# The feed-forward half of a cross-attention block as one program instead of four, with shared buffers and split DMA queues

## The chip, the cores and the metric

The kernel runs on one core of one Trainium2 chip. Its time is the device time of one execution in microseconds (us). Three runs of the kernel before gave 2516.38, 2515.7 and 2514.28 us, a median of 2515.7 us.

## What is computed

`x` is 8192 rows (4 x 2048) of 512 numbers. The first half of the reference is a layer norm and a cross-attention in which each row looks at four rows of a table; the change does not touch it. The second half is a quantised feed-forward network on the normalised rows:

```
x = act_qdq(x)                                   # 16-bit integers times one scale for the whole tensor
up = act_qdq(x @ lpbq_dequant(w_up).T)           # 512 -> 1536
gate = act_qdq(x @ lpbq_dequant(w_gate).T)       # 512 -> 1536
sig = fixed_qdq_u16(jax.nn.sigmoid(gate))
gate = act_qdq(gate * sig)
o = act_qdq(gate * up)
return o @ lpbq_dequant(w_down).T                # 1536 -> 512, added to x
```

`act_qdq` divides by a scale that is the largest magnitude of the whole tensor over 32767, and rounds. So nothing of a tensor can be rounded before all of it is known, and there are five such peaks: of h (the normalised rows), gate, gate * sig, up and o. This is what cuts the network into passes over DRAM.

## The kernel before

The 8192 rows are 16 blocks (`NB`) of 512 rows. The 1536 hidden columns of a block are three units (`UNITS`); a unit is a tile of 128 partitions x 2048 numbers, 1 MB in float32 and 0.5 MB in int16. There are 48 units (`NU`). Each product of 16-bit integers is made of three float16 matmuls (high x high, low x high, high x low), 24 matmuls of 128x512 into one pair of PSUM banks; a unit is two such pairs. With four pairs of banks (`pp`) TensorE can run four pairs ahead of the evictions. Each pass has its code in a function of its own, with its own buffers, semaphores and barrier at the end (`Scope`):

- **`feed_gate`**: TensorE makes gate; ScalarE copies each pair out of PSUM (line 980, the eviction), VectorE takes the peak of each unit (line 939), SyncE stores the raw unit (`gate_scratch`). The weights of up and down are quantised beside it.
- **`feed_up`**: TensorE makes up; eviction at line 1230, peak at line 1197, three units of raw results on chip (`raw`, kept until the next pass). Beside it the gate units come back, are rounded (`gq`, lines 1237 and 1173), and the peak of gate * sig is found (ScalarE lines 1239 and 1241, VectorE lines 1178 and 1185): this is the first phase, unit steps 0 to 31. From step 33 (`SECOND`) `READY` = 30 units get their second treatment, two per step: sigmoid (line 1249), `sq` (line 1178), and gate * sig rounded in place (line 1192). The last `KEPT` = 9 units are on chip; 21 are read back from DRAM through a ring of four buffers (`load_again`) and stored again.
- **`product_peak`**: no matmuls. For each unit VectorE takes the peak of |gate| * |up| (line 1399), from |up| made by ScalarE (line 1367) and |gate|. The 18 units without second treatment ("late") first need sigmoid (line 1353), `sq` (line 1382), `gp` (line 1385) and the rounding (line 1372). Of the 30 others ScalarE takes the magnitude of 17 (line 1358) and VectorE that of 13, in two instructions (lines 1391 and 1394). Three up units are still on chip; all gate units are loaded into six slots, the up units into five.
- **`feed_out`**: per unit ScalarE rounds up (line 1492) and o (line 1499), VectorE multiplies (line 1549) and splits o into two float16 parts (lines 1538 and 1553), TensorE does the down product (line 1571), VectorE adds the result to x1 (line 1516) and SyncE stores the block.

All loads and stores of these passes are in SyncE's queue, in the order in which the code writes them, with the waits of each in front of it: what stands behind a waiting store waits too. GpSimd does in them only the reduction of each peak over the partitions (line 760), followed by five small VectorE instructions (`quantiser`).

## Time and profile before

| | us |
|---|---|
| median of three runs | 2515.7 |
| profiled execution | 2515.36 |
| its span in the trace | 2513.5 |
| TensorE / VectorE / ScalarE busy | 2028.0 / 1773.7 / 1360.0 |
| attention and all before it | 719.3 |
| gate, its matmuls | 719.3 to 1219.4 |
| up, its matmuls | 1233.8 to 1747.5 |
| products, VectorE's work | 1788.2 to 1988.1 |
| down, its matmuls | 2008.7 to 2507.5 |

The profile is of one execution. It is read here stage by stage: a share of the whole span says little, since TensorE has no work at all in the products pass and no pause in the down pass.

### The profile page before, as it was taken

Reading aid. Unit: us, or ns where it says so; the run is one execution under the profiler, and the core shown is the slowest. Engines: PE = TensorE matmul, PEld = TensorE weight load, DVE = VectorE, ACT = ScalarE, POOL = GpSimd, SP = SyncE. Lnnn points to the kernel's source line nnn. Section 1 sums busy time; section 2 is a strip of 40 time slices with the busy share of each in tenths; the row PEclk is TensorE's granted clock in tenths of the full one; section 3 lists DMA queues with packets and bytes.
Section 4 is the critical chain, followed back from the end, with each engine's and each line's share of the span. In section 5 each row is a group of like instructions: output and inputs, shape, how many; then the busy total and the mean of one; then the engine's idle time right before and its main releaser. Section 6 shows DMA issues by size and latency. Waiting matters only on the chain. (4 is left out here: it accounts for less than half of the span.)

```text
span 2513.5 us, 25398 instructions
## 1 busy us (share of the span) xinstructions
PE 2028.0 (81%) x9560; PEld 947.4 (38%) x9560; DVE 1773.7 (71%) x1497; ACT 1360.0 (54%) x1434; POOL 463.8 (18%) x406
## 2 busy tenths in 40 slices
PE   4178888888769999999799999996000099999999
PEld 2134444444324444444344444442000044444444
DVE  8679999999824534532488888876799754688642
ACT  2536666666522322322388887534699753577530
POOL 0248888888600000000000000000000000000000
PEclk9589999999979999999899999998555599999999
DMA  7598999999355855843599995565899675555551
GB/s 268 199 371 310 338 345 344 336 343 352 150 185 181 265 211 189 267 156 138 221 328 352 345 346 213 209 257 205 340 372 379 254 269 223 198 205 205 221 233 67
DMA packets 143945, 652.94 MB, mean 260 GB/s; under 512 B 12496, under 2 KB 13008, under 8 KB 104016
## 3 DMA queue, kind: packets, MB, share of 16 engines
q1 hardware_dynamic: 133856, 514.49, 55.4%
q0 software_dynamic: 9216, 134.22, 14.2%
q10 hardware_dynamic: 752, 2.62, 0.3%
q8 instruction: 76, 1.25, 0.2%
q14 instruction: 45, 0.37, 0.0%
HBM read 452.71 MB, written 198.57 MB: 259 GB/s over the span
## 5 line engine op out<-in xcount | busy, mean ns | idle before, releaser
L1571 PE MATMUL fo_py<-kept_down,kept_gate 128*128 128x512 f16 x1536 | 457.8, 380 | 261.2 <-DVE kept_up L1553 261.2
L1275 PE MATMUL up_pp<-up_ah,kept_up 128*128 128x512 f16 x1536 | 461.2, 381 | 25.1 <-DVE up_al L1167 15.1
L994 PE MATMUL ga_pp<-ga_ah,kept_gate 128*128 128x512 f16 x1536 | 458.9, 380 | 18.9 <-DVE ga_al L899 18.9
L939 DVE TENSOR_REDUCE kept_gate_peak<-ga_raw 128x1 f32<-128x2048 f32 x48 | 109.7, 2286 | 299.0 <-ACT ga_raw L980 299.0
L1571 PEld LDWEIGHTS fo_py<-kept_down,kept_gate 128*128 128x128 f16 x1536 | 150.4, 98 | 443.3 <-DVE kept_up L1553 261.7
L1275 PE MATMUL up_pp<-up_al,kept_up 128*128 128x512 f16 x768 | 293.0, 382 | 0.0
L994 PE MATMUL ga_pp<-ga_al,kept_gate 128*128 128x512 f16 x768 | 292.1, 380 | 0.0
L1571 PE MATMUL fo_py<-kept_down,kept_up 128*128 128x512 f16 x768 | 291.6, 380 | 0.0
L980 ACT ACTIVATE ga_raw<-ga_pp 128x1024 f32<-128x1024 f32 x96 | 97.9, 1022 | 318.5 <-PE ga_pp L994 318.5
L1275 PEld LDWEIGHTS up_pp<-up_ah,kept_up 128*128 128x128 f16 x1536 | 151.1, 98 | 210.9 <-DVE up_al L1167 16.1
L994 PEld LDWEIGHTS ga_pp<-ga_ah,kept_gate 128*128 128x128 f16 x1536 | 150.7, 98 | 201.7 <-DVE ga_al L899 19.3
L673 PE MATMUL at_psO<-kept_wo,at_ahi 128*128 128x512 f16 x512 | 155.2, 385 | 35.9 <-ACT at_alo L475 31.2
L673 PE MATMUL at_psQ<-kept_wq,at_xhi 128*128 128x512 f16 x512 | 155.1, 385 | 8.6 <-DVE at_kv_rows L552 3.9
L552 DVE TENSOR_TENSOR at_kv_rows<-at_kv_rows,at_psQ 128x2048 f32<-128x2048 f32 x64 | 143.4, 2280 | 16.7 <-PE at_psQ L673 13.8
L633 POOL TENSOR_TENSOR at_kv_rows<-at_kv_rows 128x1024 f32<-128x1024 f32 x64 | 151.5, 2368 | 5.0
L1492 ACT ACTIVATE fo_uq<-fo_ui,kept_g 128x2048 int16<-128x2048 f32 x48 | 95.6, 1991 | 99.6 <-DMA fo_ui<-up_scratch 99.6
L1230 ACT ACTIVATE kept_up_raw<-up_pp 128x1024 f32<-128x1024 f32 x96 | 97.4, 1015 | 95.6 <-PE up_pp L1275 95.6
L1538 DVE CAST kept_gate<-fo_oq 128x2048 f16<-128x2048 int16 x48 | 33.3, 693 | 163.1 <-PE fo_py L1571 92.1
L1197 DVE TENSOR_REDUCE kept_up_peak<-kept_up_raw 128x1 f32<-128x2048 f32 x48 | 109.6, 2282 | 51.7 <-ACT kept_up_raw L1230 51.7
L557 DVE TENSOR_REDUCE at_raw<-at_kv_rows 128x64 f32<-128x2048 f32 x64 | 143.0, 2274 | 0.0
L1499 ACT ACTIVATE fo_oq<-fo_o,kept_g 128x2048 int16<-128x2048 f32 x48 | 95.8, 1996 | 57.8 <-DVE kept_up L1553 57.6
L1178 DVE TENSOR_SCALAR up_sq<-up_sig 128x2048 uint16<-128x2048 f32 x78 | 95.4, 1223 | 38.1 <-ACT up_sig L1241 35.0
(211 smaller groups left out, 3484.7 us busy)
## 6 DMA issues: line engine op xcount, KB each, us to landing
gate_scratch<-ga_raw SPq DMA_DIRECT2D x48, 1024.0 KB, 3.9
up_gin<-gate_scratch SPq DMA_DIRECT2D x48, 1024.0 KB, 8.6
up_scratch<-kept_up_raw SPq DMA_DIRECT2D x48, 1024.0 KB, 9.6
fo_ui<-up_scratch SPq DMA_DIRECT2D x48, 1024.0 KB, 9.4
pp_ui<-up_scratch SPq DMA_DIRECT2D x45, 1024.0 KB, 7.2
gate_integers<-up_gq SPq DMA_DIRECT2D x60, 512.0 KB, 8.8
kept_up<-gate_integers SPq DMA_DIRECT2D x48, 512.0 KB, 7.0
fo_gi<-gate_integers SPq DMA_DIRECT2D x48, 512.0 KB, 6.5
```

The costliest lines, as they stand in the source:

```text
L552: nc.vector.tensor_tensor(keys, keys, psQ[t % 2][:, :].unsqueeze(1).to_broadcast([P, W, D]), ALU.mult).then_inc(m["prod"], 1)
L557: nc.vector.tensor_reduce(raw[:, t % 2], kv[:, t % KR, :, 0:D].rearrange("p w (h e) -> p w h e", h=H), AX.X, ALU.add).then_inc(m["raw"], 1)
L633: nc.gpsimd.tensor_tensor(lower, lower, upper, ALU.add).then_inc(m["half"], 1)
L673: mm = nc.tensor.matmul(out[:, :], a[:, slot, c, :], w[b][:, c, :], start=(q == 0), stop=(q == len(todo) - 1))
L939: nc.vector.tensor_reduce(keep["gate_peak"][:, n:n + 1], raw[:, q, :], AX.X, ALU.max, apply_absolute_value=True).then_inc(m["peak"], 1)
L980: nc.scalar.activation(raw[:, q, h * 2 * BLK:(h + 1) * 2 * BLK], pp[(2 * n + h) % 4][:, :, :].rearrange("p a t -> p (a t)"), ACT.Copy).the ...
L994: mm = nc.tensor.matmul(pp[k % 4][:, h, :], wt[w][:, c, f:f + P], a[:, b % 2, :, c, :], start=(q == 0), stop=(q == len(todo) - 1))
L1197: nc.vector.tensor_reduce(keep["up_peak"][:, n:n + 1], raw[:, n % UNITS, :], AX.X, ALU.max, apply_absolute_value=True).then_inc(m["peak"], 1)
L1230: nc.scalar.activation(raw[:, n % UNITS, h * 2 * BLK:(h + 1) * 2 * BLK], pp[(2 * n + h) % 4][:, :, :].rearrange("p a t -> p (a t)"), ACT.C ...
L1275: mm = nc.tensor.matmul(pp[k % 4][:, h, :], wt[w][:, c, f:f + P], a[:, b % 2, :, c, :], start=(q == 0), stop=(q == len(todo) - 1))
L1499: nc.scalar.activation(oq[:, :], o[:, :], ACT.Copy, scale=g[:, 13:14]).then_inc(m["oq"], 1)
L1571: mm = nc.tensor.matmul(py[k % 8][:, :], a[b % 2][:, f, t * P:(t + 1) * P], wt[w][:, f, :], start=(q == 0 and i == 0), stop=(q == UNITS - ...
```

## The change

The four functions become one, `feed`, in one `Scope`: one list of instructions per engine, no barrier between the passes, and semaphores in place of it. The parts:

- Buffers are allocated once and used again under other names (`gin` holds the float weights, then the gate units, then reloaded integers; the up weights' space holds loaded up units once TensorE is through with it; `raw` serves both gate and up).
- SyncE issues only loads. GpSimd's queue issues all stores: h, raw gate, raw up, gate integers, treated units, and the output, the last block in four parts.
- The input parts of the first up block are loaded and split at the end of the gate pass; `hq` has two buffers in the up pass.
- The second treatment reads back 22 units (`KEPT` is 8 now) through nine buffers (`AR`), two per step from step 33 on, and uses them four steps later. The last nine of them and the eight kept units stay on chip for the products; ScalarE takes the magnitude of 11 of these (`DONE`) in steps 36 to 46 of the up pass.
- In the products 31 gate units are loaded (18 late, 13 others) into four slots (`WQ`), the up units into four (`UR`). `DONE` has 11, ScalarE has 13, VectorE 6. A late unit's sigmoid is made three steps ahead (four before), with one buffer each for sigmoid, `sq` and `gp` (two before).
- The first loads and the first product of the down pass do not wait for the peak of o, and VectorE splits o before it makes the next product.

```diff
+    GR, QR, AR = 4, 4, 9
+    AGAIN = READY - KEPT
+    AWAY = NU - KEPT
+    SECOND = NU - READY // 2
+    DONE = list(range(KEPT)) + [v for v in range(KEPT, READY) if v - KEPT >= AGAIN - AR][:3]
+    LOADED = AGAIN - AR
+    WQ, UR = 4, 4
...
+                def load_again(w):
...
+                        else:
+                            sp.wait_ge(again_out[w % AR], 16 * (w // AR))
+                        sp.dma_start(again(KEPT + w), gate_q[w]).then_inc(again_in[w % AR], 16)
+
+                def load_gated(i):
+                    if home[i] == "load":
+                        j, u = at_home(i), order[i]
+                        if j < WQ:
+                            sp.wait_ge(m["al"] if j < 2 else m["gpeak"], 2 * NB if j < 2 else NU)
+                        else:
+                            sp.wait_ge(m["prod"], [k for k in range(NU) if home[k] == "load"][j - WQ] + 1)
...
+                for n in range(NU):
+                    if n % UNITS == 0:
+                        load_hq(n // UNITS + 1)
+                    for u in first_units(n):
+                        load_gate(u + GR)
+                    if n >= SECOND:
+                        sp.wait_ge(m["peak"], NU + n - 1)
+                        load_again(2 * (n - SECOND))
+                        load_again(2 * (n - SECOND) + 1)
+                for i in range(-4, NU):
+                    if i + 4 < NU:
+                        load_gated(i + 4)
+                    if 0 <= i + 3 < NU:
+                        load_up(i + 3)
...
+                def store_raw(n):
+                    pool.wait_ge(m["peak"], n + 1)
+                    to, n = (gate_d, n) if n < NU else (up_d, n - NU)
+                    pool.dma_start(to[n // UNITS, n % UNITS], raw[:, n % UNITS, :]).then_inc(stored[n % UNITS], 16)
...
+                gpk_p(pool)
+                for n in range(NU):
+                    if n == SECOND:
+                        ppk_p(pool)
+                    for u in first_units(n):
+                        store_gate(u)
+                    if n >= 1:
+                        store_raw(NU + n - 1)
+                    for v in second_units(n - 1):
+                        store_gated(v)
...
+                def magnitude(v):
+
+                    if v < KEPT:
+                        act.wait_ge(kept_out[v], 16)
+                    else:
+                        act.wait_ge(again_out[(v - KEPT) % AR], 16 * ((v - KEPT) // AR + 1))
+                    nc.scalar.activation(again(v), again(v), ACT.Abs).then_inc(m["mag"], 1)
...
+                act.wait_ge(m["g_scales"], 1)
+                act.wait_ge(m["w_lo"], 2 * PIECES)
+                act.wait_ge(m["hq"], NB)
+                for n in range(NU):
+                    for u in first_units(n)[:1]:
+                        first(u)
+                    for v in second_units(n)[:1]:
+                        second(v)
+                    evict(NU + n, 0)
...
+                for b in range(2 * NB):
+                    pe.wait_ge(m["al"], b + 1)
+                    wt = keep["gate" if b < NB else "up"]
+                    if b == NB:
+                        pe.wait_ge(m["w_lo"], PIECES)
+                    for pair in range(PAIRS):
+                        k = b * PAIRS + pair
+                        need(pe, m["out"], k - 3)
```

What stands in SyncE's queue late in the up pass. Before, steps 42 and 43 (`up_gq` is the ring of four, `kept_up_raw` the raw up unit, `up_hq` the h integers):

```order
L1086 DMA up_hq<-h_integers 128x2048
L1116 DMA up_scratch<-kept_up_raw 128x2048
L1112 DMA gate_integers<-up_gq 128x2048 x2
L1105 DMA up_gq<-gate_integers 128x2048 x2
L1116 DMA up_scratch<-kept_up_raw 128x2048
L1112 DMA gate_integers<-up_gq 128x2048 x2
L1105 DMA up_gq<-gate_integers 128x2048 x2
```

A reload stood behind the store of the unit just treated, in the same buffer. After, the same engine in steps 39 to 43 and what follows (`ff_gin` and `ff_ring` are the nine buffers of the reload; `kept_up` is the up weights' space, the first load of the products):

```order
L1074 DMA ff_gin<-gate_integers 128x2048 x5
L1074 DMA ff_ring<-gate_integers 128x2048
L1051 DMA ff_hq<-h_integers 128x2048
L1074 DMA ff_gin<-gate_integers 128x2048 x4
L1085 DMA ff_hq<-gate_integers 128x2048
L1095 DMA kept_up<-up_scratch 128x2048
```

The stores have left it and the loads of the products follow at once. They are in GpSimd's queue, which held no DMA in these passes before; its last steps of the up pass and what follows:

```order
L1185 DMA up_scratch<-ff_raw 128x2048
L1197 DMA gate_integers<-ff_gin 128x2048 x2
L1185 DMA up_scratch<-ff_raw 128x2048
L1197 DMA gate_integers<-ff_gin 128x2048 x2
L760 ISA ff_u_all<-ff_u_red 128x1
L760 ISA ff_o_all<-ff_o_red 128x1
L1228 DMA out<-ff_h_parts 128x4x512 x15
L1232 DMA out<-ff_h_parts 128x512 x4
```

The reduction of up's peak (`ff_u_all`) now stands behind three stores. On VectorE the end of the products and the start of the down pass, before (`fo_o` is o, `fo_oq` its integers, `kept_gate` and `kept_up` its two float16 parts):

```order
L756 TENSOR_REDUCE fo_o_red<-kept_o_peak 128x1
L767 TENSOR_SCALAR kept_g<-fo_o_all,kept_g 128x1
L768 TENSOR_SCALAR kept_g<-kept_g 128x1
L769 RECIPROCAL kept_g<-kept_g 128x1
L770 TENSOR_TENSOR kept_g<-kept_g 128x1
L1508 TENSOR_TENSOR kept_g<-kept_g,kept_alpha 128x1
L1549 TENSOR_TENSOR fo_o<-fo_gi,fo_uq 128x2048
L1538 CAST kept_gate<-fo_oq 128x2048
L1549 TENSOR_TENSOR fo_o<-fo_gi,fo_uq 128x2048
L1553 TENSOR_TENSOR kept_up<-fo_oq,kept_gate 128x2048
```

And after (`ff_hq` is o, `ff_ring` its integers):

```order
L756 TENSOR_REDUCE ff_o_red<-kept_o_peak 128x1
L1389 TENSOR_TENSOR ff_hq<-ff_gin,ff_sig 128x2048
L767 TENSOR_SCALAR kept_g<-ff_o_all,kept_g 128x1
L768 TENSOR_SCALAR kept_g<-kept_g 128x1
L769 RECIPROCAL kept_g<-kept_g 128x1
L770 TENSOR_TENSOR kept_g<-kept_g 128x1
L1424 TENSOR_TENSOR kept_g<-kept_g,kept_alpha 128x1
L1454 CAST kept_gate<-ff_ring 128x2048
L1456 TENSOR_TENSOR kept_up<-ff_ring,kept_gate 128x2048
```

The first product has moved ahead of the scale, and no second product stands between the two halves of the first split.

## Rows read from the trace of the kernel before

**Rows 1.** Table by stretch: busy us and instructions per engine, granted clock, DMA share, GB/s.
```profile
1219.40:1233.80 14.40, 0.00 (x0) 0.00 (x0) 5.32 (x10) 1.02 (x1) 0.35 (x1) 0.62 0.49 195
1233.80:1578.00 344.20, 344.19 (x1589) 155.83 (x1590) 293.99 (x231) 275.29 (x179) 0.35 (x1) 1.00 0.88 320
1578.00:1747.50 169.50, 158.85 (x717) 70.30 (x715) 130.70 (x78) 78.16 (x55) 0.00 (x0) 0.98 0.59 223
1747.50:1788.20 40.70, 0.00 (x0) 0.00 (x0) 20.07 (x17) 10.65 (x8) 0.35 (x1) 0.56 0.62 237
1788.20:1988.10 199.90, 0.00 (x0) 0.00 (x0) 193.78 (x158) 188.75 (x100) 0.00 (x0) 0.50 0.88 348
1988.10:2008.70 20.60, 0.00 (x0) 0.00 (x0) 7.38 (x10) 7.79 (x4) 0.35 (x1) 0.50 0.87 332
2008.70:2507.50 498.80, 498.76 (x2304) 225.70 (x2304) 290.86 (x239) 247.47 (x128) 0.00 (x0) 1.00 0.53 204
2507.50:2513.50 6.00, 0.00 (x0) 0.00 (x0) 0.75 (x1) 0.00 (x0) 0.00 (x0) 0.69 0.47 175
```

**Rows 2.** Waits of TensorE and ScalarE, 1580 to 1750: us, times, longest.
```profile
PE up_pp L1275 <- ACT kept_up_raw L1230: 10.0, 4, 3.6
ACT up_sig L1249 <- DMA up_gq<-gate_integers: 61.5, 8, 9.5
```

**Rows 3.** Timeline at the end of the gate pass: start, us, engine, line.
```profile
1219.39 1.02 ACT L980 ACTIVATE ga_raw<-ga_pp 128x1024 f32<-128x1024 f32 x1 [4.16 <-PE ga_pp L994]
1220.45 2.29 DVE L939 TENSOR_REDUCE kept_gate_peak<-ga_raw 128x1 f32<-128x2048 f32 x1 [8.07 <-ACT ga_raw L980]
...
1238.18 1.28 ACT L1241 ACT_TABLE_LOAD   x1
```

**Rows 4.** Timeline at the end of the up pass.
```profile
1773.20 2.35 DVE L1192 SCALAR_TENSOR_TENSOR up_gq<-up_sq,kept_g,up_gq 128x2048 int16<-128x2048 uint16 x1
1775.47 0.20 DVE L756 TENSOR_REDUCE up_u_red<-kept_up_peak 128x1 f32<-128x48 f32 x1
1775.76 0.35 POOL L760 PARTITION_ALL_REDUCE up_u_all<-up_u_red  x1 [204.06 <-DVE up_u_red L756]
1776.14 0.21 DVE L767 TENSOR_SCALAR kept_g<-up_u_all,kept_g 128x1 f32<-128x1 f32 x1 [0.48 <-POOL up_u_all L760]
```

**Rows 5.** Groups by line in the products pass: busy, mean ns, idle before.
```profile
L1399 DVE CUSTOM_DVE_ANT_0 pp_junk<-kept_gate,pp_ua 128x2048 f32<-128x2048 int16 x48 | 109.8, 2288 | 5.0 <-DVE kept_o_peak L1399 3.1 <-ACT pp_ua L1367 1.9
...
L1385 DVE TENSOR_TENSOR pp_gp<-kept_up,pp_sq 128x2048 f32<-128x2048 int16 x18 | 41.3, 2293 | 0.6
...
L1358 ACT ACTIVATE kept_gate<-kept_up 128x2048 int16<-128x2048 int16 x17 | 32.2, 1893 | 0.0
L1382 DVE TENSOR_SCALAR pp_sq<-pp_sig 128x2048 uint16<-128x2048 f32 x18 | 22.0, 1222 | 11.1 <-ACT pp_sig L1353 11.1
L1394 DVE TENSOR_TENSOR kept_gate<-kept_up,pp_neg 128x2048 int16<-128x2048 int16 x13 | 15.9, 1226 | 0.4
L1391 DVE TENSOR_SCALAR pp_neg<-kept_up 128x2048 int16<-128x2048 int16 x13 | 8.9, 687 | 0.0
```

**Rows 6.** DMA issues: count, KB each, median us to landing.
```profile
kept_up<-gate_integers SPq DMA_DIRECT2D x48, 512.0 KB, 7.0
...
at_kv_rows<-kv_table,kept_rows POOLq DMA_INDIRECT x64, 12.7
```

**Rows 7.** Page, costliest groups: the down pass's rounding and cast.
```profile
L1538 DVE CAST kept_gate<-fo_oq 128x2048 f16<-128x2048 int16 x48 | 33.3, 693 | 163.1 <-PE fo_py L1571 92.1
...
L1499 ACT ACTIVATE fo_oq<-fo_o,kept_g 128x2048 int16<-128x2048 f32 x48 | 95.8, 1996 | 57.8 <-DVE kept_up L1553 57.6
```

**Rows 8.** Groups by line on GpSimd, whole span.
```profile
L620 POOL DMA_INDIRECT at_kv_rows<-kv_table,kept_rows x64 | 63.6, 994 | 50.0 <-DVE at_root_d L546 35.0 <-issue 10.4 <-POOL at_att L636 4.2
L653 POOL TENSOR_TENSOR at_shift<-at_nmean,at_rstd 128x2 f32<-128x2 f32 x32 | 42.7, 1334 | 2.5
...
L651 POOL TENSOR_TENSOR at_rstd<-at_root,at_root_d 128x2 f32<-128x2 f32 x32 | 8.0, 250 | 2.5
```

More of the change, by code:

```diff
@@ new lines, in feed @@
+    WQ, UR = 4, 4
+    FG, FU = 4, 3
+    hT_v = hT_d.rearrange("(b n) p d -> b p n d", n=SUB)
+    out_v = out.rearrange("(b n p) d -> b p n d", p=P, n=SUB)
+    x1_v = x1_d.rearrange("(b n) p d -> b p n d", n=SUB)
+    ready = [("kept", v) for v in (KEPT - 1, KEPT - 2, KEPT - 3)]
+    here = [("kept", v) for v in range(KEPT - 3)] + [("ring", v) for v in range(KEPT + LOADED, READY)]
+    there = [("load", v) for v in range(KEPT, KEPT + LOADED)]
+    for a, b in itertools.zip_longest(here, there):
+        ready += [e for e in (a, b) if e]
@@ new lines, in feed @@
+    waiting = list(range(AGAIN, AWAY))
+    order, made, home = [], [], []
+    for i in range(NU):
+        late = made.count("late")
+        if len(waiting) * (i + 1) // NU > len(waiting) * i // NU:
+            order.append(waiting[late])
+            made.append("late")
+            home.append("load")
+        else:
+            where, v = ready[i - late]
+            order.append(AWAY + v if v < KEPT else v - KEPT)
+            home.append(where)
+            made.append("done" if v in DONE else "dve" if made.count("act") > 2 * made.count("dve") else "act")
@@ L1049, in again, with stored_first @@
         def again(v):
[L1051 removed]
+            if v < KEPT:
+                return kept(v)
+            r = (v - KEPT) % AR
+            return wide[:, r, :] if r < 2 * GR else ring[:, 0, :]
+        def stored_first(r):
+            return len(range(r, AWAY, QR))
         def have_gq(eng, u):
```

1063 lines of the change are left out of this document (523 added, 540 removed).

## The prediction, written before the changed kernel was run

> **What bounds the kernel now.** The page's slices show TensorE near full except for a hole after three quarters of the span, so I cut the span into stages and read the table by stretch first [rows 1]. The down pass is TensorE alone: 498.8 us for 2304 matmuls, nothing else to see. That is the yardstick: 96 pairs of units of work, 5.20 us a pair, 10.4 us a unit. The up pass has as many matmuls but takes 344.2 + 169.5 = 513.7 us, 14.9 more. The rest is time without a matmul: 14.4 us between gate and up, 40.7 between up and VectorE's first product, 199.9 for the products, 20.6 until the down matmuls, 6.0 at the end. In the products VectorE is busy 193.78 of 199.9 and ScalarE 188.75, so there VectorE's list is the bound with ScalarE 5 us behind it. Second, the waits [rows 2]: in the up pass's last part TensorE waits for evictions, and the evicting ScalarE stood 61.5 us in eight waits for units reloaded from DRAM. Third, the timeline at the seams [rows 3, 4]; fourth, durations by line and DMA landings [rows 5 to 8].
>
> The sum is made against the profiled execution, 2515.4 us (span 2513.5 and 1.9 around it); the median shown is 2515.7, 0.3 above, which I neglect.
>
> **The seam between gate and up.** TensorE now goes on: the split of the first up block stands before the last two gate peaks on VectorE, and nothing else of TensorE's waits is new. But ScalarE may not evict up's first pair before it has the scale of gate and has treated unit 0. TensorE can run four pairs ahead, 4 x 5.20 = 20.8 us. The chain: last gate eviction starts 1219.4, 1.0; peak 2.3 [rows 3], to 1222.7; GpSimd first issues the raw store, which I price by its indirect DMA, 1.0 [rows 8]; reduction 0.35 and five small VectorE operations of at most 0.21 each [rows 4], to 1225.1; then on ScalarE copy and magnitude, 2.0 each by the rounding [rows 7], table load 1.3 [rows 3], sigmoid 2.0, eviction 1.0: 1233.4. TensorE needs it at 1219.4 + 20.8 = 1240.2. Cover 6.8 us, so the whole 14.4 goes. If the cover failed (all of these twice as long) some 7 us would come back.
>
> **The reload in the up pass.** The reloads no longer stand behind a store into the same buffer; they are issued four steps (41 us) ahead of a landing of 7.0 for the same tensor [rows 6]. ScalarE's waits go, and with them TensorE's. What is late next is VectorE: per step two times (1.22 + 2.35) for `sq` and treatment [rows 5, 4], a peak 2.3, a third of a split (0.69 + 1.23, [rows 7, 5]) 0.64, together 10.1 of 10.4 us. It fits, barely. ScalarE: two sigmoids 4, evictions 2, a magnitude 1.9, 7.9. The last three magnitudes read units treated one step before, whose store must land first: treated 5.9 us after an eviction, issued 1.0, landed 8 to 12.7 later, 15 to 20 against the 10.4 at which ScalarE stands there. It waits 5 to 9 us once; VectorE's next `sq` comes about 3 us later than its turn, and keeps that to the end. TensorE is covered by its four pairs. So the up pass becomes 498.8: gain 14.9, and 3 go to the tail.
>
> **The tail of up.** Let T be the last up matmul, 1747.5 before. Eviction 1.0, peak 2.3, `sq` and treatment of unit 29 3.6, reduction 0.2, GpSimd's issue of its store 1.0 (what is queued behind it is the all-reduce), 0.35 and five small operations 1.1: T + 9.5, with the lag of 3 T + 12.5. There VectorE starts on the products: the first three up units are on chip, late unit 22 was requested long before. The first loaded up unit is wanted some 6 us later and is issued at T. Before it was T + 40.7, of which 28 us were the reload ring draining and 13 the barrier and first loads. Gain 28.2. Bounds: 31.2 without lag; 20 if stores and reloads lag by a landing of 8 more.
>
> **The products.** VectorE: 13 pairs of (0.69 + 1.23) become 6 [rows 5], 7 x 1.91 = 13.4 less: 199.9 - 13.4 = 186.5, 3.9 a unit. ScalarE: 17 magnitudes of 1.9 become 13, 188.75 - 7.6 = 181. DMA: (31 x 0.52 + 45 x 1.05) = 63.5 MB, at the 348 GB/s of the stage 182 us, so still below. What is new is a ring of four for gate units, each freed only by the product of the fourth load before it. From the list in which `order` is made, that product is 5 units back in 5 of 27 cases and else 6 or 7. A late unit is wanted by the sigmoid, 2.0, three VectorE steps ahead of its own product's end: with 5 units of distance 5 x 3.9 - 2.0 - 3 x 3.9 = 5.8 us are left for issue and landing, 0.3 + 7.0 [rows 6]: a stall of 1.5. With 6 there are 9.7, none. 5 x 1.5 = 7.5: 194. Gain 5.9. Bounds: 13.4 if landing is 5 us or less; if the ring stalls all 18 late units by 1.5, 186.5 + 27 = 213.5, a loss of 13.6. I take the value between because only short distances can stall.
>
> **From products to down.** The loads are issued before the last products. Then 0.3, the first o 2.3 (the scale is ready 1.8 after the reduction, beside it), the rest of the scale 0 to 1.1, rounding 2.0, cast 0.7, low part 1.2: 7.6 against 20.6. Gain 13.0. In the down pass VectorE has for a late unit 1.2 + 2.3 + 0.7 + 1.2 + 2.3 and 4/3 sums of 0.75 [rows 1], 8.7 us of 10.4; TensorE stays the bound, 498.8.
>
> **The end.** The last store is 0.25 MB instead of 1 MB; of 6.0 us 0.75 is VectorE's. GpSimd's issue costs some of it. Gain 1, between 0 and 2.
>
> **The stores on GpSimd.** Same bytes, so no bandwidth either way. No row shows a plain store from GpSimd. Nearest is its indirect DMA: 0.99 us of GpSimd, 12.7 to landing for 2 MB [rows 8, 6]. A raw unit's buffer is wanted again three units later, 31.2 us, of which 5.2 + 1.0 + 2.3 + 1.0 are gone before the store moves: 21.7 are left for landing, against 12.7. But GpSimd and VectorE hold each other up: a tiny GpSimd operation took 1334 ns on average where its like took 250 [rows 8]. From below the new issues cost VectorE nothing, from above 0.99 each. I take 2 us in all, since an issue meets one of the short `sq` operations in about one case in four and the loser is as often GpSimd.
>
> The Trainium skill ("SBUF — State Buffer", sections "Who interferes with whom" and "A bandwidth-pool intuition that's wrong") speaks against this change: a DMA issued from GpSimd has its descriptors written by GpSimd, and a VectorE copy, cast or tensor_scalar in a two-port mode and that writing block each other fully. The 1334 against 250 agrees that they block; that it holds for descriptors no run here shows. By the rule only `sq`, the rounding and the cast are held or hold, and by its figure of 3.1 instead of 0.62 us for a blocked DMA a store would be, as an estimate, 2.5 us late, inside the 21.7 - 12.7 of room, so the sum would stay.
>
> **Sum.** 14.4 + 14.9 + 28.2 + 5.9 + 13.0 + 1.0 - 2.0 = 75.4. 2515.4 - 75.4 = 2440.
>
> **Rivals.**
> (a) *The ring of four sets the products.* For it: four slots, each freed by a product, and a sigmoid only three steps ahead, on an engine whose next work for VectorE stands behind it. Against: only distance 5 falls short of the landing measured, and 63.5 MB go in the pass instead of 48 x 0.52 + 45 x 1.05 = 72.4. Products 213.5 instead of 194: 2460. Chance 0.17.
> (b) *No stall anywhere.* Landings after the stores are gone could be 5 us, as DMA is less busy. Products 186.5, tail 9.5, no holding: 2440 - 7.5 - 3 - 2 = 2427. Chance 0.15.
> (c) *GpSimd's issues hold VectorE: slower.* Place: the up pass. First phase, per step 9.6 us of VectorE (two of three units' roundings, 1.5 `sq` and products, a peak, a third of a split) and 2.25 stores; second phase 10.1 and 3. Held 0.99 per store: 11.8 and 13.1 against 10.4; 1.4 x 32 + 2.7 x 15 = 85 us, against which the idle 10% of VectorE is already counted. 2440 - 2 + 85 = 2523, slower by 8. It decides from about 0.9 us per store on. Against: the operation held in the rows is GpSimd's [rows 8], and none shows VectorE held; nearly every store would have to hit it. Chance 0.04.
> (d) *Stores land late.* If a raw store from GpSimd takes 25 us instead of 12.7, each round of three units costs 3.3, 32 rounds 106: 2546. Nothing in the rows is near 25. Chance 0.02.
> That the barriers alone cost little would not undo the sum: what it counts is the loads and chains behind them, and these are moved.
>
> **Numbers.** Forecast 2440, chance 0.62, its own range 2430 to 2452. (a) 0.17, (b) 0.15, (c) 0.04, (d) 0.02. Range for 8 in 10: 2424 to 2466. 0.2%, about what can be told from no change, is 5 us: faster 0.94, same 0.01, slower 0.05.
>
> **What would show it.** No gap of TensorE at the seam of gate and up, and first up eviction 14 us after the last gate matmul. ScalarE's waits for reloads under 10 us in the up pass. VectorE's first product within 15 us of the last up matmul. Products near 194 with waits of `sq` for sigmoid and of sigmoid for a DMA in a handful of units; if over 205, (a). Down matmuls 8 us after the last product. `sq` near 1.22: if its mean is over 1.7 in the up pass, (c). I am wrong if TensorE stands in the up pass for evictions by more than 10 us.

## The result and the profile after

The changed kernel takes 2459.4 us (median of 4 runs, 2458.2 to 2460.3), the kernel before beside it on the same chip 2516.0 (4 runs, 2514.3 to 2519.4). The ratio is 0.9773 (95% interval 0.9756 to 0.979): faster by 2.3%. The forecast was 2440 with a range of 2424 to 2466. The profiled run took 2458.2, its span 2456.4; before it was 2513.5, so 57.1 us of span went.

First the table by stretch, cut where the stages end, as [rows 1] has it for before: gate, up, tail of up, products, products to down, down, end.

```profile
719.20:1219.30 500.10, 500.09 (x2304) 226.16 (x2305) 195.42 (x119) 134.91 (x118) 34.51 (x64) 0.99 0.58 203
1219.30:1716.80 497.50, 497.49 (x2305) 225.34 (x2303) 442.69 (x324) 382.47 (x250) 80.93 (x118) 1.00 0.82 307
1716.80:1725.90 9.10, 0.00 (x0) 0.00 (x0) 7.77 (x10) 3.02 (x2) 2.31 (x4) 0.77 0.99 336
1725.90:1937.60 211.70, 0.00 (x0) 0.00 (x0) 181.95 (x145) 184.75 (x98) 0.00 (x0) 0.50 0.83 319
1937.60:1945.50 7.90, 0.04 (x1) 0.07 (x2) 5.35 (x10) 5.27 (x3) 2.32 (x1) 0.50 0.93 317
1945.50:2445.20 499.70, 499.70 (x2304) 225.90 (x2304) 297.34 (x240) 246.49 (x128) 15.31 (x18) 1.00 0.53 203
2445.20:2456.40 11.20, 0.12 (x1) 0.00 (x0) 0.75 (x1) 0.00 (x0) 0.54 (x1) 0.66 0.10 37
```

In the up pass the busy time of TensorE is the length of the stretch: it never waits. Set against [rows 1]:

| term | forecast | measured |
|---|---|---|
| seam of gate and up, 14.4 us before | 14.4 | 14.4 |
| up pass, 513.7 before | 14.9 | 16.2 |
| tail of up, 40.7 before | 28.2 | 31.6 |
| products, 199.9 before | 5.9 | -11.8 |
| products to down, 20.6 before | 13.0 | 12.7 |
| down, 498.8 before | 0 | -0.9 |
| end, 6.0 before | 1.0 | -5.2 |
| VectorE held by GpSimd's issues | -2.0 | 0 |
| sum (0.1 lies ahead of the seam) | 75.4 | 57.0 |

Two terms missed, the products by 17.7 and the end by 6.2; the tail, the up pass and the absent holding give 6.7 back. Down and the step to it make up the remaining 1.2.

The timeline at the seam (start, duration, engine, line; in brackets how long the engine had been idle and what ended that), beside [rows 3]: the chain that decides whether TensorE must stop.

```profile
1220.61 2.29 DVE L1254 TENSOR_REDUCE kept_gate_peak<-ff_raw 128x1 f32<-128x2048 f32 x1 [8.07 <-ACT ff_raw L1479]
1223.18 0.53 POOL L1185 DMA_DIRECT2D gate_scratch<-ff_raw  x1 [9.83 <-DVE kept_gate_peak L1254]
1223.74 0.30 POOL L760 PARTITION_ALL_REDUCE ff_g_all<-ff_g_red  x1
...
1225.17 2.00 ACT L1502 ACTIVATE ff_ring<-ff_gin,kept_g 128x2048 int16<-128x2048 f32 x1 [4.60 <-DVE kept_g L1322]
...
1230.38 2.00 ACT L1506 ACTIVATE ff_sig<-ff_ring,kept_g 128x2048 f32<-128x2048 int16 x1
1232.29 1.00 ACT L1479 ACTIVATE ff_raw<-ff_pp 128x1024 f32<-128x1024 f32 x1
```

The scale is there at 1225.17 (forecast 1225.1), and the first up eviction ends at 1233.3 (forecast 1233.4); TensorE would have needed it 20.8 us after 1219.3, at 1240.1. The cover of 6.8 us was real.

The waits of the products stage (engine, tile and line that waited, for whom: us, times, longest) show where the time went:

```profile
DVE ff_sig L1415 <- ACT ff_ring L1562: 25.3, 12, 5.0
ACT ff_sig L1548 <- DMA ff_ab<-gate_integers: 9.8, 2, 5.8
ACT ff_sig L1548 <- DMA ff_hq<-gate_integers: 8.0, 4, 2.8
ACT ff_sig L1548 <- DVE ff_sq L1337: 4.3, 3, 1.7
```

VectorE (products, L1415) stands 25.3 us for ScalarE's magnitude of the up unit, and ScalarE was late since its sigmoid (L1548) had stood 17.8 us for the load of a late unit. Matched one by one with the list `order`, 16.4 of these 17.8 us are five waits of 1.6 to 5.8 us, before the five late units whose slot comes free only five units ahead; the sixth wait, 1.4, is before one of the ten late units with a distance of six. VectorE is busy 181.95 us of 211.7; before it was 193.78 of 199.9. The work shrank about as reckoned (by 11.8, forecast 13.4), and the stage grew.

Last, GpSimd's stores and the operation that was feared for, VectorE's `sq`. First `sq`, durations in ns (least, median, greatest):

```profile
L1337 DVE TENSOR_SCALAR ff_sq<-ff_sig x96: 1214/1222/1228, 1232.4 to 1926.9; 128x2048 uint16<-128x2048 f32 x96
```

Then the groups of GpSimd's issues of raw stores (busy us, mean ns):

```profile
L1185 POOL DMA_DIRECT2D up_scratch<-ff_raw x48 | 37.1, 774 | 269.0 <-DVE kept_up_peak L1254 269.0
L1185 POOL DMA_DIRECT2D gate_scratch<-ff_raw x48 | 26.5, 553 | 464.0 <-DVE kept_gate_peak L1254 464.0
```

And the stores themselves (KB, median us from issue to landing):

```profile
up_scratch<-ff_raw POOLq DMA_DIRECT2D x48, 1024.0 KB, 7.8
```

Not one of 96 `sq` operations is longer than 1228 ns; before, without stores from GpSimd, the longest was 1229. The issues themselves are longer: 774 ns on average in the up pass, where VectorE is busy 442.69 of 497.5 us, against 553 in the gate pass (195.42 of 500.1). So VectorE is not held by GpSimd's issues. That GpSimd is held by VectorE fits the longer issues; no run varies it alone.

### The profile page after: what moved, and what is told of

Same layout as the page of the kernel before. It is cut to its first block, busy times and chain, and to the rows that moved or that the text cites. A ratio compares the mean times of both kernels' runs of the same rounds, so it can differ in the third digit from the quotient of the medians.

```text
span 2456.4 us, 25419 instructions
## 1 busy us (share of the span) xinstructions
PE 2025.0 (82%) x9560; PEld 947.2 (39%) x9560; DVE 1768.4 (72%) x1482; ACT 1372.7 (56%) x1441; POOL 598.0 (24%) x607
## 4 chain that ended last, share of the span: by engine, by line
PE 61%; ACT 3%; issue 3%; DVE 3%; DMA 1%; POOL 0%; DVEq 0%; ACTq 0%; SPq 0%; POOLq 0%
PE ff_pp L1619 41%; PE ff_pp L1633 20%; ACT ff_ring L1562 1%; DVE ff_sig L1415 1%; DMA ff_hq<-gate_integers 1%; DVE ff_h_parts L1399 1%; DVE ff_sq L1337 1%; ACT ff_sig L1548 0%; ACT ff_hq L1569 0%; ACT ff_ab L1569 0%; DMA ff_ab<-gate_integers 0%; DMA ff_h_parts<-up_scratch 0%; DMA ff_ab<-hT_scratch 0%; ACT ff_gin L1566 0%; DVE ff_sq L1406 0%
## 5 line engine op out<-in xcount | busy, mean ns | idle before, releaser
L1633 PE MATMUL ff_pp<-kept_down,kept_gate 128*128 128x512 f16 x1536 | 458.6, 380 | 228.7 <-DVE kept_up L1456 228.7
L1619 PE MATMUL ff_pp<-ff_h_parts,kept_gate 128*128 128x512 f16 x2304 | 500.3, 380 | 18.8 <-DVE ff_h_parts L1249 18.8
L1619 PE MATMUL ff_pp<-ff_h_parts,kept_up 128*128 128x512 f16 x2304 | 497.4, 379 | 0.0
L1479 ACT ACTIVATE ff_raw<-ff_pp 128x1024 f32<-128x1024 f32 x192 | 195.2, 1019 | 420.3 <-PE ff_pp L1619 420.3
L1619 PEld LDWEIGHTS ff_pp<-ff_h_parts,kept_gate 128*128 128x128 f16 x2304 | 226.1, 98 | 292.9 <-DVE ff_h_parts L1249 19.2
L1619 PEld LDWEIGHTS ff_pp<-ff_h_parts,kept_up 128*128 128x128 f16 x2304 | 225.4, 98 | 271.8
L1254 DVE TENSOR_REDUCE kept_gate_peak<-ff_raw 128x1 f32<-128x2048 f32 x48 | 109.7, 2285 | 293.1 <-ACT ff_raw L1479 293.1
L1633 PEld LDWEIGHTS ff_pp<-kept_down,kept_gate 128*128 128x128 f16 x1536 | 150.6, 98 | 411.3 <-issue 231.3
L1633 PE MATMUL ff_pp<-kept_down,kept_up 128*128 128x512 f16 x768 | 292.0, 380 | 0.0
L1337 DVE TENSOR_SCALAR ff_sq<-ff_sig 128x2048 uint16<-128x2048 f32 x96 | 117.3, 1222 | 34.1 <-ACT ff_sig L1506 29.9
L1228 POOL DMA_DIRECT2D out<-ff_h_parts x15 | 13.7, 911 | 462.2 <-DVE ff_h_parts L1432 462.2
L1633 PEld LDWEIGHTS ff_pp<-kept_down,kept_up 128*128 128x128 f16 x768 | 75.4, 98 | 91.3 <-issue 1.1
## 6 DMA issues: line engine op xcount, KB each, us to landing
at_xs<-in_x SPq DMA_DIRECT2D x32, 512.0 KB, 14.3
```

The costliest lines, as they stand in the source:

```text
L1254: nc.vector.tensor_reduce(keep[to][:, k:k + 1], raw[:, n % UNITS, :], AX.X, ALU.max, apply_absolute_value=True).then_inc(m["peak"], 1)
L1337: nc.vector.tensor_scalar(sq[:, :], sig[:, a, :], 65536.0, 65535.0, ALU.mult, ALU.min).then_inc(m["sq"], 1)
L1479: nc.scalar.activation(raw[:, n % UNITS, h * 2 * BLK:(h + 1) * 2 * BLK], pp[(2 * n + h) % 4][:, :, :].rearrange("p a t -> p (a t)"), ACT.C ...
L1619: mm = nc.tensor.matmul(pp[k % 4][:, h, :], wt[w][:, c, f:f + P], a[:, b % 2, :, c, :], start=(q == 0), stop=(q == len(todo) - 1))
L1633: mm = nc.tensor.matmul(pp[k % 8 // 2][:, k % 2, :], a[b % 2][:, f, t * P:(t + 1) * P], wt[w][:, f, :], start=(q == 0 and i == 0), stop=(q ...
```

## The experiments

Each ran on the same chip as the kernel before; ratios are to it. "The changed kernel" means 2459.4 us, ratio 0.9773. In the cuts of code, `...` stands for lines left out. Profiles of single kernels are compared by stretches counted from their own last gate or up matmul, T.

**The end.** The last block's four stores from SyncE:

```diff
...
-                            pool.wait_ge(m["y"], b * SUB + t + 1)
-                            pool.dma_start(out_v[b][:, t, :], xb[:, b % 2, t, :]).then_inc(y_out[b % 2], 16)
...
+                for t in range(SUB):
+                    sp.wait_ge(m["y"], (NB - 1) * SUB + t + 1)
+                    sp.dma_start(out_v[NB - 1][:, t, :], xb[:, (NB - 1) % 2, t, :]).then_inc(y_last, 16)
...
```

> The four stores of the last block go from GpSimd's queue to SyncE's, nothing else. After the change the span ends 11.2 us after the last product of down (2445.2 to 2456.4), and in its last 7.4 us nothing moves. Theory A, the price lies in leaving the scope (the queue of GpSimd drained, some 150 semaphores cleared), whatever queue stored last: the 7 us stay, ratio to the kernel after 1.000, so 2459 us. Theory B, the price is the completion of a transfer that GpSimd issued: the end shrinks to the 6.0 us of before or less (0.25 MB moves in less time than 1 MB), a gain of 5 to 7 us, 2453 us.

Measured 2451.7 us (2449.3 to 2453.1), ratio 0.9743 (0.9726 to 0.9759). The last stretch, from the last matmul:

```profile
2442.90:2447.50 4.60, 0.12 (x1) 0.00 (x0) 0.75 (x1) 0.00 (x0) 0.00 (x0) 0.85 0.15 57
```

4.6 us instead of 11.2: the 7 us hang on GpSimd having stored last. Theory A (a price of leaving, whatever queue stored last) is wrong; B's reason is not shown, since a late completion and a slow leaving by GpSimd look alike here. A probe parts them, a tiny VectorE operation behind the landing:

```diff
+                dve.wait_ge(y_out[(NB - 1) % 2], 16 * (NB // 2 - 1 + SUB))
+                nc.vector.memset(g[:, 15:16], 0.0).then_inc(m["gp"], 1)
```

> The changed kernel with one more tiny VectorE operation that waits for the same semaphore as GpSimd's last wait, the landing of the last 256 KB; its start in the trace says when the landing was known. After the change the last store is issued at 2446.6, its data moved until 2449, and the span ends at 2456.4. Theory C: the landing is known at about 2449 to 2450, and the 7 us behind it are GpSimd's own, spent when it leaves a program in which it has issued some 230 transfers (with 18 of its own the end was 5 us shorter, and with the last stores on SyncE it lay beside TensorE): the probe starts 2 to 4 us after the last issue. Theory B: the landing of a transfer that GpSimd issued is told late: the probe starts 8 us or more after the last issue. The whole is 2459 us either way.

One run, 2459.8 us, span 2458.1. Its timeline at the end:

```profile
2448.20 0.54 POOL L1232 DMA_DIRECT2D out<-ff_h_parts  x1 [2.19 <-DVE ff_h_parts L1432]
2450.55 0.06 DVE L1466 MEMSET kept_g<- 128x1 f32 x1 [2.79 <-DMA out<-ff_h_parts]
```

The landing is known 2.35 us after the start of the issue; 7.5 us follow in which no engine computes or moves anything. Theory C holds: the landing is not late, the program is left late. The timeline leaves out what GpSimd's instruction queue does there; asked by its line, it shows one instruction, DRAIN, that takes most of the 7.5 us. In the probe, in the run with the last stores on SyncE, and in the run of the section "The queue of the stores" in which GpSimd issues 19 transfers (durations in ns, then the start):

```profile
L1020 POOLq DRAIN  x1: 5941/5941/5941, 2450.7 to 2450.7; - x1
...
L1021 POOLq DRAIN  x1: 7660/7660/7660, 2413.0 to 2413.0; - x1
...
L1020 POOLq DRAIN  x1: 1612/1612/1612, 2454.4 to 2454.4; - x1
```

With the last stores on SyncE this instruction starts with GpSimd's last issue, 34 us before the end, and lies beside TensorE: it still takes 7.66 us, but nobody waits for it.

**Reload buffers.** Four instead of nine, stores on GpSimd as changed:

```diff
-    GR, QR, AR = 4, 4, 9
+    GR, QR, AR = 4, 4, 4
...
-    DONE = list(range(KEPT)) + [v for v in range(KEPT, READY) if v - KEPT >= AGAIN - AR][:3]
+    DONE = list(range(KEPT))
...
-                        load_again(2 * (n - SECOND))
-                        load_again(2 * (n - SECOND) + 1)
+                        for w in range(AGAIN):
+                            if SECOND + w // 2 + (3 if w >= AR else 0) == n:
+                                load_again(w)
```

> Four reload buffers instead of nine, with the reloads issued as early as the four slots permit and no magnitudes of the last three at the end of the up pass. Theory 1, the nine buffers made the up pass run without a stop: the last 15 steps of the up pass are again held by reloads, ScalarE waits for them 20 to 40 us in 1560 to 1717, TensorE waits some 10 to 15 us, and the up pass is about 510 us instead of 497.5. Rival, the stores that went to GpSimd's queue did it: the up pass stays within 2 us of 497.5. The products get longer in either case, since 18 finished units instead of 13 come through the ring of four (36 loads instead of 31) and three magnitudes more are computed there: by 5 to 15 us. Sum 2474 to 2487 by theory 1, 2464 to 2475 by the rival.

Measured 2496.0 us (2492.5 to 2499.4), ratio 0.9917 (0.9899 to 0.9935): above what either theory allowed. Up pass and products:

```profile
1219.30:1716.80 497.50, 497.50 (x2306) 225.34 (x2303) 441.40 (x323) 375.05 (x246) 80.11 (x118) 1.00 0.80 304
1727.85:1975.40 247.55, 0.00 (x0) 0.00 (x0) 183.80 (x147) 188.61 (x100) 0.00 (x0) 0.50 0.72 284
```

The waits for reloads are back, and TensorE does not notice:

```profile
ACT ff_sig L1515 <- DMA ff_gin<-gate_integers: 31.0, 13, 4.4
```

So theory 1 falls: the nine buffers are worth nothing in the up pass. They are worth 35.9 us in the products (247.55 against 211.7), where five units more must come through the ring of four and three magnitudes more are computed; I had priced that at 5 to 15. With 36 units through four slots, 13 loads have a distance of only four units (none has in the changed kernel), and ScalarE's sigmoids stand 51.4 us for loads there instead of 17.8.

**The queue of the stores.** All stores of the gate and up passes back in SyncE's queue, nine buffers:

```diff
                     for u in first_units(n):
                         load_gate(u + GR)
+                        store_gate(u)
+                    if n >= 1:
+                        store_raw(NU + n - 1)
+                    for v in second_units(n - 1):
+                        store_gated(v)
...
-                        load_again(2 * (n - SECOND))
-                        load_again(2 * (n - SECOND) + 1)
+                        for w in range(AGAIN):
+                            if SECOND + w // 2 + (2 if w >= AR else 0) == n:
+                                load_again(w)
```

and likewise in the gate pass, where the load of up's first block goes ahead of the last two raw stores. Reloads from the tenth on are issued two steps later than in the changed kernel, so that the queue does not wait for itself.

> All stores of the gate and up passes go back into SyncE's queue between the loads (those of the output stay on GpSimd); nine reload buffers and the order of the engines' work stay, and reloads from the tenth on are issued two steps later, so that the queue does not lock itself. With four reload buffers and the stores on GpSimd the up pass stayed at 497.5 us, so the nine buffers alone did not give the 15 us there. Theory 1: either remedy is enough alone, nine buffers or a queue of their own for the stores; then this one too has an up pass of 497 to 500 us and 2457 to 2463 us as a whole. Rival: the queue is what counts, and stores that wait among the loads hold the reloads up even with nine buffers: ScalarE waits over 40 us for reloads, the up pass is over 505 us, the whole over 2467.

Measured 2459.3 us (2459.0 to 2461.5), ratio 0.9776 (0.976 to 0.9792): no difference from the changed kernel. The up pass took 497.5 us again, and ScalarE waited for no reload. Two differences nearly cancel. Tail and products take 12.1 + 216.3 us instead of 9.1 + 211.7, since the first load of the products stands behind the last stores:

```profile
1727.74 2.00 ACT L1547 ACTIVATE ff_sig<-ff_hq,kept_g 128x2048 f32<-128x2048 int16 x1 [11.10 <-DMA ff_hq<-gate_integers]
```

and the end is 6.7 us instead of 11.2: the last store is issued at 2451.98, from GpSimd as in the changed kernel, and the span ends at 2457.5. With the 2.35 us to landing of the probe, 3.2 remain instead of 7.5, and DRAIN, shown above, takes 1.61 instead of 5.94. In `feed` GpSimd issues 19 transfers here instead of 201.

**Both together**, four buffers and SyncE's queue (the two diffs above, with the reloads issued as under "Reload buffers"):

> Stores of both passes in SyncE's queue and four reload buffers together, as the kernel before had it, but inside the one program and with the seam kept. Theory 1 (the two remedies cover each other): now ScalarE's waits for reloads are near the 61.5 us of before, TensorE waits some 10 us for evictions, the up pass is 505 to 514 us and the tail behind it T + 15 to 30 instead of T + 9 to 11; the products as with four buffers 247 us; the whole 2508 to 2525. Rival: the 15 us of before came from the separate program of the up pass, its own barrier and pipeline start, and not from reloads: the up pass stays under 501 us and the whole under 2500.

Measured 2498.2 us (2496.8 to 2501.9), ratio 0.9932 (0.9916 to 0.9949): inside the rival's bounds. Up pass 497.5 us, TensorE waits 0.3, ScalarE 32.9 for reloads. Neither the number of buffers nor the queue, nor the two together, is what the kernel before suffered from. Left are the rival's reason (the program of its own) and where in the queue a reload stands. This edit, on top of the last run, moves only the latter:

```diff
+                    if n == SECOND:
+                        for w in range(AR - 1):
+                            load_again(w)
...
-                    if n >= SECOND:
-                        for w in range(AGAIN):
-                            if SECOND + w // 2 + (3 if w >= AR else 0) == n:
-                                load_again(w)
+                    for v in [v for v in second_units(n - 1) if v >= KEPT]:
+                        load_again(v - KEPT + AR - 1)
```

> As the kernel with four reload buffers and all stores in SyncE's queue (up pass 497.5 us, TensorE waited 0.3), but each reload is issued as the kernel before did it: directly behind the store of the unit three before it, half a step of 10.4 us to one step before it is wanted, instead of a whole step and more. Theory: this place in the queue made the 61.5 us of ScalarE's waits and the 10 us of TensorE's in the kernel before; so now ScalarE waits 50 to 70 us for reloads, TensorE 8 to 15 us, the up pass is 505 to 514 us, and the whole is 2498 plus 10 to 35 us (the tail of up too). Rival: something else of the old program did it (its start, its own buffers); the up pass stays under 500 us and the whole under 2503.

Measured 2535.4 us (2533.8 to 2537.6), ratio 1.0071 (1.0056 to 1.0087): slower than the kernel before, and 37 us slower than its twin. Waits from 1580 to 1760 (to the end of the reloads), and the two stretches up pass and tail:

```profile
ACT ff_sig L1514 <- DMA ff_gin<-gate_integers: 73.0, 10, 8.6
...
PE ff_pp L1619 <- ACT ff_raw L1479: 10.7, 5, 3.9
```
```profile
1217.70:1734.00 516.30, 504.49 (x2305) 226.20 (x2303) 430.40 (x317) 368.80 (x242) 0.70 (x2) 0.99 0.79 293
1734.00:1767.50 33.50, 0.04 (x1) 0.00 (x0) 20.13 (x17) 8.65 (x7) 0.35 (x1) 0.54 0.63 235
```

This is the picture of [rows 2]. Counted to the end of the reloads, ScalarE waits 77.7 us in ten waits before and 73.0 in ten here (61.5 and 56.7 to just behind the last up matmul); TensorE 10.0 and 10.7; the up pass is 513.7 and 516.3 us. ScalarE's waits, the up pass and the whole (2 us above 2533) are all a little over what the theory allowed, and the program of its own is not needed for the loss. Whether so late an issue costs the same with the stores in GpSimd's queue was not run.

How much earlier the twin issues can be read off the issues and the sigmoids of the traces, and it is less than the expectation says. In the twin the reloads that share the ring are issued between 0.8 us after and 6.5 us before the moment at which ScalarE wants them, and its waits are 5.7 us at most. With this edit, and in the kernel before alike, every second one is issued 1.1 to 3.4 us after that moment, and ScalarE waits 6 to 9.5 us each time. On average these come 2.2 us too late instead of 0.4 us ahead: 2.6 us of issue time make the difference. Why TensorE feels the one and not the other is an estimate: a step is 10.4 us and ScalarE's own work in it 6 to 7.9, so 2.5 to 4.4 us of waiting per step are free; the twin waits 3.7 per step, this run 7.3.

**The seam.** The split of up's first block goes back behind the gate's scale:

```diff
-                    if n == NU - 2:
-                        split(NB)
...
+                split(NB)
                 gate_integers(1)
```

> The split of the first block of the up pass goes back behind the gate's scale (VectorE), as the old barrier had it; no barrier comes back. Theory: TensorE stands from 1219.3 until the scale is there (1225.2) and the split of about 2 to 3 us behind it is done, some 9 us, and all of it is lost since TensorE has no other wait in the up pass: 2467 to 2469 us. Rival: what the seam gained came from the loads that start early and not from the split; then less than 3 us are lost: up to 2462 us.

Measured 2469.3 us (2469.1 to 2469.8), ratio 0.9812 (0.9795 to 0.9828), 10 us more than the changed kernel. The wait:

```profile
PE ff_pp L1618 <- DVE ff_h_parts L1249: 7.7, 1, 7.7
```

Of the 14.4 us of the seam 7.7 belong to this one edit; no run parts the rest, the barrier and the first loads. The up pass behind the gap took 499.0 instead of 497.5.

**The ring of four.** Six slots, with the discarded products moved to PSUM to make room:

```diff
-    WQ, UR = 4, 4
+    WQ, UR = 6, 4
...
-        junk = sig[:, 1, :]
+        junk = t_pp[:, 0:4, :].rearrange("p a t -> p (a t)")
...
-            return hq[:, j % WQ, :] if j % WQ < 2 else ab[:, j % WQ - 2, :]
+            j %= WQ
+            return (hq, ab, shorts(t_sig[:, :, :])[:, 2:4])[j // 2][:, j % 2, :]
```

> Six slots instead of four in the ring through which the products take their loaded units; the room is that of the second sigmoid buffer, which held only the discarded products, and these go to the free PSUM banks. Products took 211.7 us with VectorE busy 182 and ScalarE 185. Theory 1, the ring of four is what VectorE waits for (25.3 us for the sigmoids that stand behind a load, 8 us more of ScalarE for the slots): products 188 to 197 us, the whole 2440 to 2447. Rival, the waits come from the single sigmoid buffer and the three steps of lookahead, and the ring only shows them: products stay over 205 us, the whole above 2453. Second rival, the DMA share (0.83) is the floor: about 200 us.

Measured 2443.5 us (2441.3 to 2445.2), ratio 0.9705 (0.9689 to 0.9721). Products stage and VectorE's wait there:

```profile
1727.56:1924.30 196.74, 0.00 (x0) 0.00 (x0) 183.48 (x145) 184.54 (x98) 0.00 (x0) 0.50 0.90 344
```
```profile
DVE ff_pp L1417 <- ACT ff_ring L1564: 8.3, 7, 1.8
```

The products are 15.0 us shorter, of 17.7 missed. ScalarE's wait for loads falls from 17.8 us to 2.3, and the DMA share rises from 0.83 to 0.90, so 0.83 was no floor. The control uses the freed room for a second sigmoid buffer instead:

```diff
-                        sigmoid_integer(NU + READY + x, 0)
+                        sigmoid_integer(NU + READY + x, x % 2)
...
-                        act.wait_ge(m["sq"], NU + READY + x)
-                        nc.scalar.activation(sig[:, 0, :], gated(k)
+                        act.wait_ge(m["sq"], NU + READY + max(x - 1, 0))
+                        nc.scalar.activation(sig[:, x % 2, :], gated(k)
```

> Ring of four as it was; the discarded products go to the free PSUM banks, and their room serves as a second sigmoid buffer in the products. With six slots and one sigmoid buffer the products went from 211.7 to 196.7 us. Theory 1, the ring: only the 4.3 us that ScalarE stands for the sigmoid buffer can go, products 205 to 212, the whole 2453 to 2460. Rival, the free room as such (PSUM for the junk, or the sigmoid buffer) and not the slots gave the 15 us: products under 200 and the whole under 2448.

Measured 2458.5 us (2455.8 to 2460.3), ratio 0.9769 (0.9753 to 0.9786); products 211.7 us as in the changed kernel. It is the slots, not the room.

**How long a slot is held.** One constant, on ScalarE in the products:

```diff
-                AHEAD = 3
+                AHEAD = 2
```

> The changed kernel with one constant other: ScalarE treats a late unit in the products two steps ahead of its product instead of three; ring of four, SyncE's order and the end as they are. In the trace of the changed kernel a loaded slot is held from the sigmoid's start to the product's end for 17.8 us (1825.8 to 1843.7) and over 21 in the next case, where the prediction reckoned with 13.7; with issue and landing (0.3 + 4.8) a slot comes round in 23 to 27 us, against the 24 that four of 31 loads in 48 products of 3.9 us may take. Theory (the holding time is what the ring lacks): one step less is 3.9 us less of it, the loads have landed when the sigmoid is wanted, and the products go from 211.7 towards the 196.7 of the ring of six: 197 to 205 us, the whole 2444 to 2453. Rival: the lead is used up by VectorE, which then waits for each of the 18 sigmoids instead (rounding ready too late, 1 to 2 us each): products 208 to 225, the whole 2455 to 2473.

Measured 2440.8 us (2440.3 to 2441.5), ratio 0.97 (0.9684 to 0.9716): 18 us better than the changed kernel, 3 us below the theory's range. The products:

```profile
1725.90:1919.60 193.70, 0.00 (x0) 0.00 (x0) 182.32 (x144) 184.14 (x98) 0.00 (x0) 0.50 0.87 349
```

In the timeline of the changed kernel one late unit's slot is held from the first of these rows to the end of the second:

```profile
1825.83 2.00 ACT L1548 ACTIVATE ff_sig<-ff_hq,kept_g 128x2048 f32<-128x2048 int16 x1 [2.09 <-DMA ff_hq<-gate_integers]
...
1841.38 2.29 DVE L1415 CUSTOM_DVE_ANT_0 ff_sig<-ff_hq,ff_ring 128x2048 f32<-128x2048 int16 x1 [1.17 <-ACT ff_ring L1562]
...
1843.70 0.32 SPq L1085 DMA_DIRECT2D ff_hq<-gate_integers  x1
```

The third row is the next load into that slot. With two steps ahead, a slot is held from here to here:

```profile
1786.12 1.99 ACT L1548 ACTIVATE ff_sig<-ff_ab,kept_g 128x2048 f32<-128x2048 int16 x1
...
1798.16 2.28 DVE L1415 CUSTOM_DVE_ANT_0 ff_sig<-ff_ab,ff_ring 128x2048 f32<-128x2048 int16 x1
```

17.8 and 14.3 us; over all 18 late units, each sigmoid's start to its product's end, the mean is 20.3 us and 15.6. The next load waits for that end, then lands in a median of 4.3 to 4.8. ScalarE's wait for loads falls from 17.8 us to 3.9. The rival's price, VectorE waiting for the sigmoids, is 2.6 us in all.

**Combinations.** Ring of six, SyncE's end, and a second sigmoid buffer in PSUM:

```diff
...
+        two = [sig[:, 0, :], t_pp[:, 4:8, :].rearrange("p a t -> p (a t)")]
...
-                        nc.scalar.activation(sig[:, 0, :], gated(k)
+                        nc.scalar.activation(two[x % 2], gated(k)
```

> Ring of six, a second sigmoid buffer in PSUM, the discarded products in PSUM, and the last block's stores from SyncE. Alone the ring gave 16 us and the end 7. Products: ScalarE busy 184.5 of 196.7 and VectorE 183.5; with the 4.7 us wait for the sigmoid buffer gone 190 to 195. Whole 2443.5 - 7.5 - 4 = 2432, range 2428 to 2438. If the two engines merely hand their waits on, the products stay at 196.7 and the whole is 2436.

Measured 2444.6 us (2443.7 to 2446.3), ratio 0.9717 (0.9701 to 0.9733): no better than the ring alone. The same operation by where it reads:

```profile
L1341 DVE TENSOR_SCALAR ff_sq<-ff_sig x87: 1215/1223/1228, 1231.8 to 1909.9; 128x2048 uint16<-128x2048 f32 x87
L1341 DVE TENSOR_SCALAR ff_sq<-ff_pp x9: 2285/2286/2289, 1737.1 to 1918.1; 128x2048 uint16<-128x2048 f32 x9
```

Nine readings from PSUM cost 9 x 1.06 = 9.6 us of VectorE, which in the products is on the path (204.8 us instead of 196.7). Without that buffer (the ring's and the end's diffs together):

> Ring of six with one sigmoid buffer, discarded products in PSUM, last block's stores from SyncE; the second sigmoid buffer in PSUM is left out, since VectorE read it at 2286 ns instead of 1223 (nine of them, 9.6 us more of VectorE in the products, 204.8 us instead of 196.7). Expected: products 196.7 and the short end, 2443.5 - 7.5 = 2436 us, range 2433 to 2440. If the two gains hide each other, over 2441.

Measured 2438.2 us (median of 5, 2436.0 to 2439.6), ratio 0.9679 (0.9666 to 0.9693): the fastest version run, 3.2% under the kernel before. Products 197.6 us, end 4.8. The one constant with SyncE's end was not run; as an estimate from the two single results it would be some 2433.

## Why the prediction was right, and where it was not

The forecast case (faster, no engine held, TensorE never stopped in the up pass) came true, and the time lay inside the range; 2459 is 19 above the forecast and on the number of rival (a), 2460. That the whole falls on that number is luck: the end missed by 6.2 us and three other terms gave 6.7 back.

- *Seam.* Right to 0.1 us at both points of the chain. Undoing the early split shows 7.7 of the 14.4 as its own.
- *Up pass.* Right in size (16.2 for 14.9) and in the reason given, a reload no longer behind a store and issued early. The lead was not 41 us throughout: 50 to 54 us for the first nine reloads, 22 to 35 for the others. And the words "four steps ahead" rest on nine buffers, which the experiments show were not needed for the up pass: four buffers do it in either queue, with issues from 0.8 us too late to 6.5 us ahead, 31 to 33 us of ScalarE's waits left and none of TensorE's for an eviction. With every second issue 2.6 us later, 73 us of waits reach TensorE.
- *Tail.* T + 9.1 for T + 12.5. The chain without lag was T + 9.5, and the lag of 3 us did not come: ScalarE waited 4.6 us once for a store, and nothing of that was left at T.
- *Products.* The failed step is "a late unit is wanted by the sigmoid, 2.0, three VectorE steps ahead of its own product's end". That gives a slot held 2.0 + 3 x 3.9 = 13.7 us. The trace has 20.3 on average. Between the sigmoid and the product three steps ahead ScalarE still has its own magnitude (2.0), and VectorE the product behind it (2.3), which makes 18, and whatever lead ScalarE has on VectorE comes on top.

  A second error went the other way: the load was priced at 0.3 + 7.0, and in the five waits at distance five the sigmoid starts 3.5 to 3.7 us after the slot came free. With 13.7 and 3.6 nothing would have stalled, since 5 x 3.9 - 13.7 = 5.8 us are left; that was rival (b)'s case, and its fast landings came and its 186.5 did not. With 20.3 held, distance five is short by 0.8 + 3.6 = 4.4 us and distance six (3.1 left) by 0.5. Measured are 3.3 on average at distance five, and at distance six one wait of 1.4 in ten. So that "only short distances can stall" was nearly right, and the size was not: 16.4 us at ScalarE for 5 x 1.5 = 7.5, and 25.3 at VectorE, since the magnitude it needs stands behind the waiting sigmoid.

  Rival (a) had the size right, 213.5 for 211.7, by an upper bound in which all 18 late units stall by 1.5; six stalled. As a mechanism it was mine with the wrong holding time, and 0.17 was too little for it. Six slots give 196.7, a shorter hold 193.7, against a forecast of 194. That these meet the forecast is luck too: they have 2.3 and 3.9 us of waits for loads left, not 7.5, and the other 7 to 10 us above 186.5 lie elsewhere in the hand-over between the two engines, which no run takes apart.
- *Products to down, and down.* 7.9 for 7.6, and 499.7 for 498.8.
- *End.* The step "GpSimd's issue costs some of it. Gain 1, between 0 and 2" failed: I priced the size of the last store and GpSimd's issue, and not that the program is left 7.5 us after the landing, 5.94 of them in GpSimd's DRAIN. Nothing in the rows of the end before showed it, since SyncE had stored there.
- *GpSimd's issues.* I took 2 us off and it was 0. What the Trainium skill ("SBUF — State Buffer", "Who interferes with whom") says, that of a VectorE operation in a two-port mode and GpSimd whichever comes first holds the shared ports and the other is blocked, shows here on one side at most. VectorE was never the one held: `sq` is 1214 to 1228 ns throughout. For GpSimd's side the trace agrees, 774 against 553 ns. The 3.1 against 0.62 us of its section "A bandwidth-pool intuition that's wrong" appears nowhere in these rows: an issue is 0.53 us at the least and 1.17 at the most. Rivals (c) and (d) fell: up stores landed in 7.8 us.

## What to carry to other kernels

The time a ring's slot is held runs from the first reader to the last one, counting both engines' work in between, not from the step in which the data is nominally due. Starting earlier on data makes a ring in effect shorter: one step less of lookahead was worth as much here as two more slots (2440.8 and 2443.5 us). A wait that a loader causes is set by when its issue comes: here less than 3 us on every second issue decided, where neither five more buffers nor a second queue were needed, so before buying either, move the issue. And an end must be read for what each queue still has to do after its last byte: here GpSimd, with many transfers behind it, was a bad choice for the last one.

## What the runs showed of the hardware that was not expected

- A program in which GpSimd had issued 201 transfers and also the last ones ended 7.5 us after their landing was known, 5.94 of them in one DRAIN of GpSimd; with 19 transfers it was about 3.2 us and 1.61; with SyncE storing last the whole end, from the last matmul, was 4.6. In the kernel before, GpSimd's DRAIN at the end of a pass in which it issued no transfer was 0.47. That the number of transfers since the last DRAIN sets it is suggested by these three points and not shown.
- The issue of a plain 1 MB store took GpSimd 0.55 us on average in the gate pass (VectorE busy 39%) and 0.77 in the up pass (89%); the stores landed in a median of 7.0 and 7.8 us.
- VectorE's scale-and-clamp of 128x2048 float32 takes 1223 ns from SBUF and 2286 from PSUM, while writing discarded float32 products to PSUM instead of SBUF cost next to nothing (48 of them, with the ring of six: VectorE busy 183.48 us in the products against 181.95).
